# Routed experts of a graph-and-mixture network: sums in two tables by the expert's parity, weights asked for at an add, row numbers copied apart

## The reference, cut to what matters

```python
# first layer: 16 routed experts of width 256, top 4 of them a token; 2 shared experts
def _L0_ffn_ref(...):
    gate_probs = jax.nn.softmax(x @ gate_w.T, axis=-1)
    top_v, top_i = jax.lax.top_k(gate_probs, TOP_K)          # TOP_K = 4
    top_v = jax.nn.softmax(top_v, axis=-1)
    combine = jnp.einsum('tk,tke->te', top_v, jax.nn.one_hot(top_i, E, dtype=x.dtype))
    for e in range(E):
        routed = routed + combine[:, e:e + 1] * _mlp(x, re_w1[e], re_b1[e], re_w2[e], re_b2[e])
    ...
    return routed + shared / SHARED
# second layer: 16 routed experts of width 384 with a gated activation (768 columns up), top 2; 1 shared
...
x = x + _L0_ffn_ref(_layernorm(x), ...)
...
x = x + _L1_ffn_ref(_layernorm(x), ...)
```

## Time and profile before

| what | value |
|---|---|
| time, median of 3 runs | 2367.56 us (2363.34 to 2369.09) |
| time of the profiled execution | 2370.24 us |
| its span | 2368.2 us |
| mean granted clock of TensorE | 0.971 of full |
| TensorE busy | 2173.5 us, 92% |
| VectorE, ScalarE, GpSimd busy | 42%, 21%, 12% |
| routed experts of the first layer | some 833 to 1104 us |
| routed experts of the second layer | some 2107 to 2358 us |

### The profile page before, as it was taken

How to read it: one execution, slowest core, us unless ns; L and a number is a source line. 1 busy time by engine, 2 the same in 40 slices (tenths; PEclk the granted TensorE clock), 3 DMA queues, 4 the chain that set the end, 5 groups by cost and what they waited for, 6 DMA issues and landing times. The chain is left out here.

```text
span 2368.2 us, 26639 instructions
## 1 busy us (share of the span) xinstructions
PE 2173.5 (92%) x7344; PEld 1249.5 (53%) x7345; DVE 1003.9 (42%) x2731; ACT 508.1 (21%) x903; POOL 286.6 (12%) x317
## 2 busy tenths in 40 slices
PE   6998889999998988884999989999999999989997
PEld 3444444445455454442544468864478854535554
DVE  7966778302015522112124465511255413725543
ACT  2112221110103022222210144311153212201111
POOL 1200000000000044443210000000000010013333
PEclk9999999999999999997999999999989999999998
DMA  4003000000003257677200000010000001248774
GB/s 125 1 0 117 1 1 18 1 18 0 0 1 126 67 130 175 148 171 165 67 1 4 23 36 1 1 62 0 8 28 1 1 5 57 84 156 243 234 238 97
DMA packets 77201, 154.57 MB, mean 65 GB/s; under 512 B 10217, under 2 KB 21524, under 8 KB 77116
## 3 DMA queue, kind: packets, MB, share of 16 engines
q1 hardware_dynamic: 59452, 113.06, 14.5%
q0 software_dynamic: 17664, 40.43, 8.6%
HBM read 119.50 MB, written 36.18 MB: 66 GB/s over the span
## 5 line engine op out<-in xcount | busy, mean ns | idle before, releaser
L1933 PE MATMUL bank<-arena 125*125 125x257 f32 x1600 | 355.8, 383 | 4.7 <-DVE arena L1852 4.7
L1933 PEld LDWEIGHTS bank<-arena 125*125 125x125 f32 x1600 | 302.2, 189 | 60.5 <-DVE arena L1852 6.3
L2182 PE MATMUL bank<-arena 128*128 x832 | 260.3, 448 | 12.4 <-issue 6.6
L990 PE MATMUL bank<-arena 125*128 125x500 f32 (+1 forms) x720 | 253.5, 513 | 3.1 <-ACT arena L1019 2.3
L481 PE MATMUL bank<-arena 128*125 128x512 f32 x480 | 212.6, 592 | 2.1 <-ACT arena L558 1.0
L2182 PEld LDWEIGHTS bank<-arena 128*128 128x128 f32 x832 | 153.7, 195 | 111.1 <-issue 61.5
L1727 PE MATMUL bank<-arena 128*125 128x512 f32 x480 | 207.8, 592 | 1.0 <-PEq L408 1.0
L990 PEld LDWEIGHTS bank<-arena 125*128 125x128 f32 x720 | 135.5, 189 | 121.1 <-issue 109.7
L2202 PE MATMUL bank<-arena 128*128 x360 | 178.7, 627 | 7.8 <-ACT arena L2259 7.7
L2307 DVE TENSOR_TENSOR arena<-bank,arena 128x384 f32<-128x384 f32 (+1 forms) x104 | 51.6, 497 | 264.6 <-PE bank L2182 248.5
L1911 ACT ACTIVATE arena<-arena 125x625 f32<-125x625 f32 x160 | 134.5, 900 | 102.4 <-DVE arena L1852 102.2
(11 more groups left out here) (332 smaller groups left out, 2259.7 us busy)
## 6 DMA issues: line engine op xcount, KB each, us to landing
arena<-in_L_ffn_expert_w SPq DMA_DIRECT2D x16, 1536.0 KB
arena<-in_L_ffn_re_w SPq DMA_DIRECT2D x32, 512.0 KB
arena<-in_L_ffn_expert_w SPq DMA_DIRECT2D x16, 768.0 KB
arena<-in_L_mix_Wqkv SPq DMA_DIRECT2D x6, 1024.0 KB, 16.3
arena<-in_L_gnn_W SPq DMA_DIRECT2D x3, 2048.0 KB, 8.4
arena<-in_L_ffn_expert_b SPq DMA_DIRECT2D x16, 384.0 KB
token_rows<-arena SPq DMA_DIRECT2D x2, 2500.0 KB
arena<-in_L_gnn_W SPq DMA_DIRECT2D x3, 1024.0 KB, 5.5
```

The lines of the kernel that those rows point to most:

```text
L990: last = pe.matmul(st.bank[4 + n % 4][:, 0:cn], h[s][:, f * P:(f + 1) * P], st.counts[:, s, c0:c0 + cn], start=(s == 0), stop=(s == NT - 1))
L1933: return pe.matmul(st.bank[n % OUTS][0:TS, 0:ONCOL], prob[:, u % 2, s, j * TS:(j + 1) * TS], st.slots[:, head + 1, s, :], start=(s == 0), ...
L2182: last = pe.matmul(st.bank[UP[b][h]][:, 0:WP], xt[b][:, k, :], rt.ring[:, bass.ds(r, 1), k * W + h * WP:k * W + (h + 1) * WP].rearrange("p ...
```

## The change

**Two tables.** In the first layer `token_sums` gets twice as many rows, all cleared. Results of even experts are added to the first table (which also gets x and the shared part), those of odd experts to the second. `find_places` works out the parity of each tile's expert, SyncE copies these numbers to three more partitions, and `know_rows` adds them to the row numbers. `landed_by` is computed from the expert before the last, so that an add is ordered only against experts of two and more back. At the end both tables are read back and VectorE joins them, tile by tile, before it takes the moments. The second layer keeps one table and its order.

**Weights asked for later.** In both layers SyncE waits for `add_begun` instead of `down_ready`, with the same number `done_by`.

**Row numbers copied apart.** In both layers the number to gather by is copied by itself, a tile ahead (`know_get`, after the rows of the tile two back have come), and the number to add by in its own copy (`know_add`, once the add of two tiles back has landed).

```diff
@@ -1033,6 +1033,7 @@
     top, shared, shared_weight, swiglu = 4, 2, 0.5, False
+    sum_tables = 2
     slots, early = P, 3
@@ -1043,6 +1044,7 @@
     top, shared, shared_weight, swiglu = 2, 1, 1.0, True
+    sum_tables = 1
     slots, early = P, 1
@@ -1163,6 +1165,8 @@
     spare_row = ar.take(1)
+    TWO = kind.sum_tables == 2
+    other_table = ar.take(TILES) if TWO else None
     first_rows = rt.first_rows
@@ -1217,6 +1221,7 @@
         down_ready, down_added = sem("down_ready"), sem("down_added")
+        other_ready, other_spread = sem("other_ready"), sem("other_spread")
         block = ctx.enter_context(nc.Block())
@@ -1236,6 +1241,9 @@
                          comb[:, :, 0:NE]).then_inc(table_set, 16)
+            if TWO:
+                sp.wait_ge(other_ready, 1)
+                sp.dma_start(other_table[TS:P, :], other_table[0:P - TS, :]).then_inc(other_spread, 16)
             for t in range(NT):
@@ -1456,6 +1464,14 @@
             link(dve.tensor_copy(rt.expert_of, expert_f))
+            if TWO:
+                link(dve.tensor_scalar(lap, expert_f, 0.5, -0.25, ALU.mult, ALU.add))
+                link(dve.tensor_scalar(lap, lap, 12582912.0, None, ALU.add))
+                link(dve.tensor_scalar(lap, lap, -12582912.0, -2.0, ALU.add, ALU.mult))
+                link(dve.tensor_tensor(lap, lap, expert_f, ALU.add))
+                link(dve.tensor_scalar(other_table[0:TS, :], lap, float(st.table_rows), None, ALU.mult))
+                dve.nop().then_inc(other_ready, 1)
             for r in range(RING_EXPERTS, NE, RING_EXPERTS):
@@ -1463,8 +1479,10 @@
-            link(dve.tensor_tensor(ended, ended, bcast_mid(ends, 2 * MAX_PAIRS), ALU.mult))
-            link(dve.tensor_reduce(lap, ended, AX_X, ALU.max))
+            back = kind.sum_tables - 1
+            link(dve.tensor_tensor(ended[:, :, back:], ended[:, :, back:], bcast_mid(ends[:, 0:NE - back], 2 * MAX_PAIRS), ALU.mult))
+            link(dve.tensor_reduce(lap, ended[:, :, back:], AX_X, ALU.max))
             for odd in range(2):
@@ -1602,6 +1620,9 @@
                                               op0=ALU.mult, op1=ALU.add))
+                if TWO:
+                    dve.wait_ge(other_spread, 16)
+                    link(dve.tensor_tensor(to_row, to_row, other_table, ALU.add))
                 link(dve.memset(rt.row_of[:, 0:AHEAD, 0:1], 0))
@@ -2041,8 +2062,10 @@
+    more_sums = rt.ring.rearrange("p r n -> p (r n)")[0:TS, 0:NT * D].rearrange("p (t d) -> p t d", t=NT)
     weight = ar.take(TILES)
-    own_row = [ar.take(2).bitcast(I32) for _ in range(2)]
+    get_row, add_row = ([ar.take(1).bitcast(I32) for _ in range(2)] for _ in range(2))
     if SW:
@@ -2055,12 +2078,14 @@
         sums_read, summed = [sem(f"sums_read{h}") for h in range(2)], sem("summed")
+        more_read, joined = [sem(f"more_read{h}") for h in range(2)], sem("joined")
         rows_turned, xt_placed, rows_used = sem("rows_turned"), sem("xt_placed"), sem("rows_used")
...
         row_copied, all_added, first_copied = sem("row_copied"), sem("all_added"), sem("first_copied")
+        get_copied = sem("get_copied")
         add_begun, gather_begun = sem("add_begun"), sem("gather_begun")
@@ -2081,7 +2106,8 @@
                 if e >= R:
-                    sp.wait_ge(down_ready, sp.value_load(rt.done_by[0:1, e - R:e - R + 1], min_val=1, max_val=TILES + 1))
+                    sp.wait_ge(add_begun, sp.value_load(rt.done_by[0:1, e - R:e - R + 1], min_val=1, max_val=TILES + 1))
                 load_expert(sp, rt, kind, ins, e)
@@ -2089,41 +2115,54 @@
                     load_tiles(sp, st.res3, sums[1:NODES + 1, :], t0, t1, sums_read[h])
+                    load_tiles(sp, more_sums, sums[st.table_rows + 1:st.table_rows + NODES + 1, :], t0, t1, more_read[h])
                 load(sp)
-                sp.wait_ge(sums_read[0], 32)
-                sp.wait_ge(sums_read[1], 32)
+                for h in range(2):
+                    sp.wait_ge(sums_read[h], 32)
+                    sp.wait_ge(more_read[h], 32)
...
-            def know_row(b, pair):
-                pool.tensor_copy(own_row[b], pair).then_inc(row_copied, 1)
+            def know_get(g, b):
+                pool.tensor_copy(get_row[b], rt.row_of[:, bass.ds(g + AHEAD, 1), 1:2].rearrange("p a w -> p (a w)")
+                                 ).then_inc(get_copied, 1)
+            def know_add(g, b):
+                pool.tensor_copy(add_row[b], rt.row_of[:, bass.ds(g + AHEAD, 1), 0:1].rearrange("p a w -> p (a w)")
+                                 ).then_inc(row_copied, 1)
...
                 pool.wait_ge(rows_used, g + 3)
-                pool.wait_ge(row_copied, g + 2)
+                pool.wait_ge(get_copied, g + 1)
                 pool.nop().then_inc(gather_begun, 1)
...
                     out=rows[b], out_offset=None, in_=rt.table,
-                    in_offset=bass.IndirectOffsetOnAxis(ap=own_row[b][:, 1:2].bitcast(mybir.dt.uint32), axis=0)
+                    in_offset=bass.IndirectOffsetOnAxis(ap=get_row[b].bitcast(mybir.dt.uint32), axis=0)
                     ).then_inc(rows_loaded[b], 16)
             def add_rows(g, b):
+                pool.wait_ge(row_copied, g + 2)
                 pool.wait_ge(y_made, g + 3)
...
                 pool.indirect_dma_start(
-                    out=sums, out_offset=bass.IndirectOffsetOnAxis(ap=own_row[b][:, 0:1].bitcast(mybir.dt.uint32), axis=0),
+                    out=sums, out_offset=bass.IndirectOffsetOnAxis(ap=add_row[b].bitcast(mybir.dt.uint32), axis=0),
                     in_=y[b], in_offset=None, compute_op=ALU.add, **bounds).then_inc(landed[b], 16)
-            def tile(i, g, b):
+            def tile(i, g, b, last=False):
                 earlier = [pool.value_load(rt.landed_by[odd][0:1, bass.ds(g, 1)], min_val=16, max_val=16 * TILES)
...
-                pool.wait_ge(rows_loaded[b], i * 16 + (48 - 16 * b))
                 pool.wait_ge(landed[b], i * 16 + (16 - 16 * b))
-                know_row(b, rt.row_of[:, bass.ds(g + AHEAD, 1), :].rearrange("p a w -> p (a w)"))
+                know_add(g, b)
                 gather(g, b)
+                if not last:
+                    pool.wait_ge(rows_loaded[1 - b], i * 16 + 48)
+                    know_get(g + 1, 1 - b)
                 for odd in range(2):
@@ -2140,9 +2179,14 @@
             pool.wait_ge(rt.sums_set, 16 * NT)
+            know_get(0, 0)
             for g in range(2):
-                know_row(g, rt.row_of[:, g + AHEAD, :])
+                know_add(g, g)
+                pool.wait_ge(rows_loaded[g], 32)
                 gather(g, g)
+                if g:
+                    pool.wait_ge(rows_loaded[0], 48)
+                know_get(g + 1, 1 - g)
                 if g:
@@ -2151,7 +2195,7 @@
                     tile(i, i * 2 + (2 - b), b)
-            tile(more, more * 2 + 1, 1)
+            tile(more, more * 2 + 1, 1, last=True)
             for b in range(2):
@@ -2350,6 +2394,10 @@
                     dve.wait_ge(sums_read[h], 32)
+                    dve.wait_ge(more_read[h], 32)
+                    for t in range(*tiles):
+                        dve.tensor_tensor(st.res3[:, t, :], st.res3[:, t, :], more_sums[:, t, :], ALU.add).then_inc(joined, 1)
+                    dve.wait_ge(joined, tiles[1])
                     row_moments(dve, st, range(*tiles), summed)
@@ -2382,7 +2430,9 @@
         st.table = nc.dram_tensor("token_rows", (TABLE, ROW), F32, kind="Internal").ap()
-        st.sums = nc.dram_tensor("token_sums", (TABLE, D), F32, kind="Internal").ap()
+        st.sums = nc.dram_tensor("token_sums", (2 * TABLE, D), F32, kind="Internal").ap()
+        st.table_rows = TABLE
         st.made_rows = [(st.table, ROW), (st.sums, D)]
```

## The result

The changed kernel takes 2412.94 us (median of 4 runs, 2411.51 to 2417.33) against 2368.22 us of the kernel before on the same chip: a ratio of 1.0196, 95% interval 1.0177 to 1.0216. It is 44.7 us slower, where +30 was forecast (2398 us, range 2370 to 2424). The profiled execution took 2412.18 us, 41.9 more than that of before.

A forecast was written before the change was run, and what follows sets the result against it. TensorE, busy 2173.5 of 2368.2 us, was taken to bound the kernel, so only its stalls could give time back. Terms 1.0 - 32 + 15.6 + 45.6 = +30 us on the median 2367.56 gave 2398 us, range 2370 to 2424.

The forecast's parts named there:

- The direction: Whole kernel: slower, by +30 us to 2398 us; slower was given 86%, faster 8%.
- the second layer: Second layer's experts: weights asked later leave TensorE waiting 33.0 us in six stalls; +45.6 us in all with slow clock.
- The cold clock: Second layer: after each of six stalls TensorE runs slow, 2.4 us each, +14.5 us.
- The third rival: Second layer's weights in time: only experts 5 and 13 wait, 2.9 us each, +3.9; total 2356 us, faster; 8%.
- Reloading and joining: End of first layer: four more transfers and five joins on VectorE, +15.6 us, between +13 and +18.
- The front: Start of first layer: five links on VectorE count in full, the larger clearing is hidden; +1.0 us.
- Two tables in the first layer: First layer's tile loop: adds wait only for experts two back, removing 32 of 39 us of stalls; bounds 39 and 10.
- the 4.8 that I named for right and the 5.2 for wrong: First layer, steps of y: near 4.8 us would show the forecast right, staying above 5.2 us wrong.
- The copies apart: Second layer: GpSimd mostly waits for VectorE, so a copy of 0.2 us is hidden; nothing.
- The crowded DMA: First layer: freed adds only crowd the DMA, gain 10 us instead of 32, total 2420 us; 13%.
- The warm rival: Both layers: TensorE's clock stays warm and the first layer gives all 39 us; +9, total 2376 us; 14%.

The follow-up runs named there:

- two pairs of runs: Late request in both layers against the first layer alone: with two tables 2412.94 and 2371.34 us, with one table 2399.54 and 2357.93 us.
- The thin pair: Kernel before, and two tables (late request in first layer), each loading a sixteenth of first-layer expert weight columns from fourth expert on: 2348.55 us and 2363.85 us.
- the kernel with its count from one: Changed kernel with its count of begun adds started at one in the second layer, so weights are asked one tile earlier: 2375.89 us, ratio 1.0035.

## Why the prediction was right and wrong

**The direction, and the second layer: right.** The reading that the change lies in a line that both layers share, and that `add_begun` starts at 0, carried the forecast. It gave stalls of 33.0 us and measured were 32.3; of 10.7 each for experts 5 and 13 and measured were 11.77 and 11.25; of 2.9 each for 3, 6 and 12 and measured were 3.66, 2.05 and 3.60. That the sums agree so well is partly luck: one stall of 2.9 did not come, and the five others are 2.2 us longer than forecast. The cold clock was put at 14.5 us for six stalls; the five slow products hold 10.3, 2.1 each, also after waits of 2.05 and 3.6 us. The term was +45.6 and came out as +41.2 in the profile and 41.6 by two pairs of runs. The missing stall is expert 14's: its weights were asked for at 2348.97 and are not awaited at 2356.34, so that the tile there is still expert 13's. I had given that expert two tiles and it has three at least. The third rival's own arithmetic is roughly borne out too: with one tile more of lead the second layer costs 2375.89 - 2371.34 = 4.6 us (two sets of runs; 4.0 by the loops of y, 233.2 against 229.2), against the 3.9 that it named.

**Reloading and joining: right.** +15.6 was forecast, +14.8 measured. The thin pair holds the same: from the last y of the first layer to the first of the second it is 1025.7 us with one table and 1040.9 with two, 15.2 more. As said there, nothing covers it.

**The front: too small.** +1.0 was forecast and the first y is 3.5 us later. One pair of profiles would not show so little, but all do: the first y stands at 842.0 us on average in eight kernels with one table (839.0 to 844.4), at 845.6 in six with two (843.8 to 846.6). The wait of TensorE did grow by the chain's length, from 0.15 to 1.29 us. What I left out is what comes behind it. TensorE's products there, kernel after:

```profile
798.52 5.37 PE L1355 MATMUL bank<-arena 128*125 128x512 f32 x8 [1.29 <-DVE arena L1636]
...
804.87 3.71 PE L1355 MATMUL bank<-arena 128*125 128x512 f32 x8
```

The product behind the wait takes 5.37 us and the next of its kind 3.71, and the granted clock of 797 to 804 us is 0.76 where it was 1.00 before. I had argued from one wait of 1.20 us that was followed by a full clock that short waits are free. In the kernel with the copies alone, without that chain, the same product waits 0.17 us and takes 3.67. All six kernels with two tables have a wait of 1.28 to 1.32 us there and then 5.37.

**Two tables in the first layer: the step that failed.** The prediction took off 32 us and the loop gave 17.3. The failed step is the sentence on what remains: an add would be "about 0.8 us late once a burst, which y's second buffer absorbs". Two things in it were wrong. First, the landing in a burst was taken as 8.2 us, from an add that the old request put behind the burst's start by 2.4 us. The new request stands right at an add, which then meets the whole of the transfer: 10.3 us in the timeline above and 10.6 at most in the first layer of the kernel with only that layer's request late. (With two tables and the old request the longest is 9.5, so 8.2 was too low for a burst there as well.) Second, y's two buffers absorb nothing here, for it is the buffer that is waited for. The waits of the kernel after from 836 to 1092 us (us, times, longest) show the chain:

```profile
ACT arena L2317 <- POOL arena L2134: 95.7, 30, 5.5
...
POOL arena L2134 <- DMA token_sums<-arena: 34.8, 13, 4.0
```

GpSimd's wait for the landing two tiles back, 34.8 us in 13 bursts, is what took the place of the 65.5 us of the earlier trace rows. It comes with the late request and not with the tables: it is 35.2 us, 13 times, with one table and the late request, and 0.8 us, once, with two tables and the old one. The waits of y for GpSimd's copy were there before the change, too. The prediction called y's second buffer a reason why GpSimd's waits were not yet a loss; the view of y in the kernel before (first layer, us, times) shows y waiting all the same:

```profile
POOL arena L2100: 85.8, 26
```

A smaller part is a wait that the change brought itself: the copy of the next gather's numbers waits for gathered rows ahead of the add (1.94 us at 933.38). It is 8.3 us in the kernel after, and 23.4 us in 12 waits with two tables and the old request:

```profile
POOL arena L2130 <- DMA arena<-token_rows,arena: 23.4, 12, 3.4
```

What two tables would give without these copies was not run. Of the gathers the forecast was fair: TensorE's waits for rows fell from 23.0 to 13.0 us.

Below this lies a mistake of attribution. I wrote that "the burst of weights, not the order alone, makes gather and add long", and then gave nearly all of their removal to the order. The thin runs part them: without bursts the loop of one table is within 5.5 us of that of two. The transfer is the cause. I take the adds' order and y's buffer to be two places where it is felt, so that freeing one leaves the other; the waits above fit this, and no run frees y's buffer alone. The two edits don't add up either: the late request gains 11.4 us with one table and nothing with two. The steps of y, 5.09 us, fell between the 4.8 that I named for right and the 5.2 for wrong.

**The copies apart: right** at nothing, by both runs, which have one table. With two tables it stays open.

**The rivals.** The crowded DMA (gain 10, 2420 us) had half of the matter: adds come free and still share the engines with weights. The loop's gain lies between its 10 and my 32, and the time, 2412.9, between the two. The warm rival fell: the clock did not hold, even behind the wait of 2.05 us. With the forecast's own terms replaced by the measured ones the sum is 3.5 - 17.3 + 14.8 + 41.2 = +42.2, where the profiled execution has +41.9. The forecast of +30 was 12 too low: 14.7 by the tables and 2.5 by the front, less 4.4 of the second layer and 0.8 of the reload, which were put too high. That it is not further off is in part because these errors lie on opposite sides.

## What to carry to other kernels

When a loop stalls once for each large load, thin that load in one run before rebuilding what waits: one such kernel told here that 38 us hung on the transfer, and a second that only 5 more were left for the second table. A large transfer asked for later and in two parts, a tile apart, was worth 26 us with a few lines, some 15 of them by the split; the table, its join and its copies gave nothing. And a wait that is moved in a shared function is priced in each of its callers: the same line gained 11 us in a layer with three tiles an expert and cost 42 in one with fewer than two.

## What the runs showed of the hardware

The length of a gap did not tell by itself what the granted clock would do. A wait of 1.29 us for VectorE was followed by a product of 5.37 us in place of 3.7, and waits of 2.05 and 2.18 us for weights (the latter in the kernel with its count from one) by 4.52 and 4.54 in place of 2.75. But the product behind a wait of 1.20 us before and those behind 1.40 us (count from one) and 2.27 us (two tables, thin weights) took 2.84. Behind the longest waits of the kernel after, 11.77 and 11.25 us, the product took 5.03 and 5.48, up to 1 us more than behind those of 2.05 to 3.66.

An accumulating indirect DMA of 128 rows landed in 4.6 to 5.5 us with thin weights and one table, and in up to 10.6 beside a transfer of 1.15 MB.
